# Five places instead of three for attention terms in the opening round, and one weight split moved from VectorE to GpSimd

## The chip, the cores and the metric

The kernel runs on one core of one Trainium2 chip. The metric is the time of one execution on the device in microseconds (us), as the median of several runs. The engines are named as in the profile: PE (TensorE), DVE (VectorE), ACT (ScalarE), POOL (GpSimd) and SP (SyncE, which here only issues transfers).

## What is computed

Sixteen sequences of 256 tokens with 512 features pass through two conditioned transformer layers. Cut to what matters:

```python
# layer 0: 16 heads of 32, keys and values through a latent of 128, window 64 in blocks of 128
proj = t_emb @ W_ada.T + b_ada                       # scale, shift of each sequence
h = layernorm(x) * (1 + scale) + shift
q = rope(h @ Wq.T);  c = h @ Wkd.T;  k = rope(c @ Wku.T);  v = c @ Wvu.T
x = x + softmax(q k^T / sqrt(32), masked) v @ Wo.T
# layer 1: 8 heads of 64, one key and value head, full attention, then the feed-forward part
h = rms(x) * ln1_w * (1 + cond @ ln1_tw.T)
x = x + softmax(rope(h Wq^T) rope(h Wk^T)^T / 8) (h Wv^T) @ Wo.T
h = rms(x) * ln2_w * (1 + cond @ ln2_tw.T)
out = x + (silu(h @ Wg.T) * (h @ Wu.T)) @ Wd.T       # 2048 wide
```

Matrices are multiplied as sums of fp16 products: each fp32 operand is split into a high half (its fp16 value) and a low half (what is left), and a product is three matmuls, high x high, high x low and low x high.

## The kernel before

The sequences go in pairs, eight rounds in all. A round runs layer 0 and layer 1 of its pair; the feed-forward part of the pair before is cut into parts that PE does between the attention steps of the round, by the table `PLAN`. Round 0, called the opening here, has no pair before it. In its place the opening prepares weights: each weight matrix is loaded into one of four staging slots in `inner_t` (or two more in `ring`), scaled by 64 and split into its two fp16 halves. `at_start(n)` is true for this round alone.

Each engine has its own instruction stream, in an order fixed by the Python code, and the streams meet in semaphores. Nothing is reordered on the chip.

Attention is done in units (table `UNIT`): 24 in layer 0, 16 in layer 1, for both sequences alternately. In layer 0 the units 0 to 7 are four heads of the first 128 queries against 128 keys each; the units 8 to 23 are two heads of the second 128 queries against 193 keys each. A unit j goes through these steps:

- PE: scores into one of four PSUM banks (in the opening preceded by a matmul that adds the mask, L1515); it needs the bank free, that is the low half of the unit that had it before
- DVE: the minimum of each row (`lows`, L1112 or L1121)
- ACT: exponentials with their sums (`exps`, L879), then the high half into `prob` (`prob_highs`, L888). Before the latter it waits in `turned_before` until the transpose that last read this place of `prob` has landed
- DVE: the low half into `prob` (`prob_lows`, L1128), and after it the minimum of unit j + 2
- SP: a DMA transpose of both halves out of `prob` (`turn_probs`, L583) into one of five places: four of `prob_t` and one in `x_mid` or `q_t`, once the product of unit j - 5 is done
- PE: the product with the values, four units later (`unit_values`, L1451 to L1453)

`prob` has `SLOTS = 3` places; unit g, counted through both layers, uses place g % 3. After the last unit of a sequence comes the normalisation (L1174, L1176), a transpose on PE, and the output projection with `wo0` or `wo1` (`finish`, `project`); DVE adds the result to x in `x_mid` (L1188), ACT sums squares (L1024) and POOL takes the root (`root`, L695 and L698), which DVE needs for the next layer.

The preparation of weights in the opening is dealt out as follows. `PIECE_OF` lists pieces of 512 columns: two for `kv`, four for `wq0`, four for `wo0`, one for `wkv1`. Pieces 0 to 5 have their high halves made by ACT, pieces from `DVE_PIECES = 6` on by DVE (L1396), and all low halves by DVE (L1400). `PIECES_AT` says before which step. The matrices of `BIG` are split by POOL alone (`big_some`): twelve instructions each, four for the high half (L780), four that scale the staged copy (L783) and four for the low half (L787); `SPLIT_AT` says at which step, and `big_split` counts those that are done, in the order of `BIG`. `split_wait` is how PE waits for a weight and SP for a stage that is to be loaded again: on `raw_split` for a matrix in pieces, on `big_split` for a big one.

`x_res` keeps the residual for the feed-forward part. It is written at the start of round 1, so in the opening it is unused but for four rows-of-16 scratch areas: `mod_copy[k]`, copies of the conditioning products k = 0 to 3 that PE then transposes. The matrices of these products are `ada0`, `ada1`, `tw1` and `tw2`.

## Time and profile before

| | us |
|---|---|
| median of 3 runs | 1775.21 |
| lowest, highest | 1773.86, 1775.33 |
| the profiled execution, its own time | 1777.36 |
| its span in the trace | 1775.60 |
| PE busy | 1705.9 (96%) |
| DVE busy | 1149.6 (65%) |
| ACT busy | 944.0 (53%) |
| POOL busy | 396.4 (22%) |

The span is the time from the first to the last instruction of the trace. Busy time is time in which an engine executes; register, branch and DMA-issuing instructions aren't counted. "Idle before <-X" behind an instruction says how long its engine had stood still and what ended it. The opening reaches from 0 to about 190 us of the span. In it, layer 0's attention units run from 50 to 99 us, layer 1's from 138 to 170.

### The profile page before, as it was taken

The page shows a single profiled execution, that of the slowest core. Times are in us where ns is not written, and L with a number is a line of the kernel's source. Part 1 is how long each engine was busy: PE and PEld are TensorE (multiplying, and loading weights), DVE is VectorE, ACT ScalarE, POOL GpSimd, SP SyncE. Part 2 cuts the span into 40 slices and gives each one's busy share as a digit, 9 for nine tenths or more (in the row PEclk, how much of TensorE's full clock was granted, in tenths as well). Part 3 has the DMA queues.
Part 4 walks back from the last instruction along what each step waited for, and adds up shares of the span by engine and source line. Part 5 has one row for each costly group of instructions (what it writes and reads, how often), then busy time and mean ns, then how long its engine had stood idle before and what let it go on. Part 6 is the DMA issues. An engine that isn't in the chain of part 4 may idle for free.

```text
span 1775.6 us, 37783 instructions
## 1 busy us (share of the span) xinstructions
PE 1705.9 (96%) x12440; PEld 930.8 (52%) x12440; DVE 1149.6 (65%) x2858; ACT 944.0 (53%) x2769; POOL 396.4 (22%) x556
## 2 busy tenths in 40 slices
PE   6676999999999999999999999999999999999999
PEld 2344545555555555555455555555555554555444
DVE  6758666676768667685676766686676856767320
ACT  3836466354755538464573547555384645735320
POOL 3438496021111011111110211110111111102120
PEclk9788999999999999999999999999999999999999
DMA  7876499353876449571793638763485817935310
GB/s 246 151 192 119 129 236 246 90 100 99 179 150 112 92 115 192 113 137 55 164 185 87 103 98 177 152 113 90 115 193 114 137 56 169 190 84 98 109 64 24
DMA packets 527227, 234.24 MB, mean 132 GB/s; under 512 B 476336, under 2 KB 493744, under 8 KB 527024
## 3 DMA queue, kind: packets, MB, share of 16 engines
q1 hardware_dynamic: 511472, 175.09, 49.6%
q10 hardware_dynamic: 15552, 56.63, 10.3%
q8 instruction: 104, 1.70, 0.4%
q14 instruction: 99, 0.81, 0.1%
HBM read 90.09 MB, written 16.78 MB: 60 GB/s over the span
## 4 chain that ended last, share of the span: by engine, by line
PE 75%; DMA 3%; DVE 3%; POOL 2%; issue 2%; ACT 1%; SPq 0%; DVEq 0%; ACTq 0%; POOLq 0%
PE up L1451 8%; PE up L1453 8%; PE up L1452 8%; PE gate L1451 8%; PE gate L1453 8%; PE gate L1452 8%; PE y L1453 4%; PE y L1451 4%; PE y L1452 4%; PE bank L1451 3%; PE bank L1453 3%; PE bank L1452 3%; DMA prob_t<-prob 2%; PE bank L1478 2%; PE bank L1486 1%
## 5 line engine op out<-in xcount | busy, mean ns | idle before, releaser
L879 ACT ACTIVATE bank<-bank,low 128x128 f32<-128x128 f32 (+2 forms) x768 | 302.5, 395 | 66.2 <-DVE low L1121 33.2
L704 POOL TENSOR_TENSOR inner_t<-inner,inner_t 128x512 f16<-128x512 f32 x128 | 150.9, 1179 | 640.0 <-ACT inner_t L1060 640.0
L1128 DVE TENSOR_TENSOR prob<-bank,prob 128x512 f16<-128x512 f32 (+1 forms) x320 | 202.8, 634 | 53.6 <-ACT prob L888 52.7
L888 ACT ACTIVATE prob<-bank 128x512 f16<-128x512 f32 (+1 forms) x320 | 178.3, 557 | 72.8 <-DMA prob_t<-prob 44.5
L1406 DVE SCALAR_TENSOR_TENSOR silu<-silu,gate 128x512 f32<-128x512 f32 x128 | 87.9, 686 | 170.9 <-ACT silu L1054 170.1
L1451 PE MATMUL gate<-mlp,ring 128*128 128x512 f16 x512 | 193.9, 379 | 1.6 <-DVE silu L1406 1.4
L1451 PE MATMUL up<-mlp,ring 128*128 128x512 f16 x512 | 193.8, 379 | 0.4 <-DVE inner L1416 0.4
L1453 PE MATMUL gate<-mlp,ring 128*128 128x512 f16 x512 | 194.0, 379 | 0.0
L1452 PE MATMUL gate<-mlp,ring 128*128 128x512 f16 x512 | 193.9, 379 | 0.0
L1453 PE MATMUL up<-mlp,ring 128*128 128x512 f16 x512 | 193.9, 379 | 0.0
L1452 PE MATMUL up<-mlp,ring 128*128 128x512 f16 x512 | 193.9, 379 | 0.0
L879 ACT ACTIVATION_READ_ACCUMULATOR bank<-bank,low 128x1 f32 x768 | 157.0, 204 | 0.0
L1054 ACT ACTIVATE silu<-gate 128x512 f32<-128x512 f32 x128 | 76.5, 598 | 125.0 <-PE gate L1453 124.6
L1117 DVE CUSTOM_DVE_ANT_0 bank<-bank,mask 128x128 f32<-128x128 f32 (+1 forms) x448 | 133.2, 350 | 1.1 <-PE bank L1522 1.0
L1024 ACT ACTIVATE work<-x_mid 128x512 f32<-128x512 f32 x64 | 40.3, 630 | 170.4 <-DVE x_mid L1188 170.4
L1060 ACT ACTIVATE inner_t<-inner 128x512 f16<-128x512 f32 x128 | 80.7, 631 | 92.7 <-DVE inner L1416 91.8
L1416 DVE SCALAR_TENSOR_TENSOR inner<-up,silu 128x512 f32<-128x512 f32 x128 | 88.2, 689 | 52.6 <-PE up L1453 42.8
L1451 PE MATMUL y<-v_hi,prob_t 128*128 128x32 f16 (+2 forms) x1024 | 109.3, 185 | 0.9 <-DMA prob_t<-prob 0.5
L1452 PE MATMUL y<-v_lo,prob_t 128*128 128x32 f16 (+2 forms) x1024 | 108.3, 184 | 0.0
L1453 PE MATMUL y<-v_hi,prob_t 128*128 128x32 f16 (+2 forms) x1024 | 108.2, 184 | 0.0
L1451 PE MATMUL bank<-wo_hi,act_hi 128*128 128x512 f16 x256 | 98.2, 383 | 1.3 <-DVE act_lo L1102 1.3
L1452 PE MATMUL bank<-wo_lo,act_hi 128*128 128x512 f16 x256 | 98.2, 384 | 0.0
(182 smaller groups left out, 4021.7 us busy)
## 6 DMA issues: line engine op xcount, KB each, us to landing
ring<-wgu_dram ACTq DMA_DIRECT2D x108, 512.0 KB, 3.9
x_in<-x_dram SPq DMA_DIRECT2D x18, 512.0 KB, 3.9
x_res<-x_mid SPq DMA_DIRECT2D x16, 512.0 KB, 3.1
wgu_dram<-ring SPq DMA_DIRECT2D x16, 512.0 KB, 3.6
out_dram<-x_res SPq DMA_DIRECT2D x32, 256.0 KB, 2.2
prob_t<-prob SPq DMA_TRANSPOSE x256, 3.5
inner_t<-wd_t_dram SPq DMA_DIRECT2D x4, 1024.0 KB, 9.3
ring<-wg_t_dram SPq DMA_DIRECT2D x16, 256.0 KB, 4.2
```

Source lines behind the costliest of these rows:

```text
L704: pool.tensor_tensor(inner_t[:, 1, f, :], inner[:], inner_t[:, 0, f, :], ALU.subtract).then_inc(inner_low, 1)
L879: ins = act.activation(bank_[:, at:at + wid], bank_[:, at:at + wid], ACT.Exp, bias=low[:, j % BANKS, k:k + 1], scale=-1.0, accum_out=total)
L888: act.activation(terms(prob[:, g % SLOTS, 0, :], layer, j), terms(work_bank[USE[f"unit{layer}", j] % BANKS][:], layer, j), ACT.Copy).then_ ...
L1054: act.activation(silu[:], gbank[:], ACT.Tanh, scale=0.5 / WS).then_inc(tanh_done, 1)
L1060: act.activation(inner_t[:, 0, f, :], inner[:], ACT.Copy).then_inc(inner_high, 1)
L1117: ins = dve.tensor_tensor_reduce(out=view, in0=view, in1=mask[:, 0:wid], scale=1.0, scalar=3.0e38, op0=ALU.add, op1=ALU.min, accum_out=low ...
L1128: dve.tensor_tensor(terms(prob[:, slot, 1, :], layer, j), terms(work_bank[USE[name] % BANKS][:], layer, j), terms(prob[:, slot, 0, :], lay ...
L1406: dve.scalar_tensor_tensor(silu[:], silu[:], 1.0, gbank[:], ALU.add, ALU.mult).then_inc(gated, 1)
L1416: dve.scalar_tensor_tensor(inner[:], ubank[:], 0.5 * HS / (WS * WS), silu[:], ALU.mult, ALU.mult).then_inc(inner_ready, 1)
L1451: pe.matmul(out_ap, left[0], right[0], start=start, stop=False)
L1452: pe.matmul(out_ap, left[0], right[1], start=False, stop=False)
L1453: return pe.matmul(out_ap, left[1], right[0], start=False, stop=stop)
```

## The change

Six edits. (1) In the opening alone there are five places for the terms, `OPEN_SLOTS = 5`: the three of `prob` and two more in the first half of `x_res`, seen as fp16 (`more_prob`). `prob_place` gives the place of a unit, `turned_before` waits by five or three. In round 1, the first units wait for the transposes of the opening that last read places 0 to 2. (2) POOL zeroes the two new places as well (`prob_clear` counts to 2). (3) `mod_copy` uses the second half of `x_res` alone, so that k = 0 and 2 share a place, as do 1 and 3. (4) `wo0` is no longer in `PIECE_OF`; piece 6 is `wkv1`, still before `unit0_18`. (5) `wo0` is in `BIG`, between `wq1` and `wo1`, and POOL splits all three at the step `fill0.0`. (6) `big_views` knows the new key.

```diff
-PIECES_AT = {"first": range(0, 2), "lat.0": range(2, 6), "unit0_9": range(6, 7), "unit0_11": range(7, 8),
-             "unit0_14": range(8, 9), "unit0_16": range(9, 10), "unit0_18": range(10, 11)}
-BIG = ["wq1", "wo1", "wd2", "wd0", "wd1", "wd3"]
-SPLIT_AT = {"fill0.0": BIG[:2], "out0a.0": BIG[2:3], "unit1_0": BIG[3:4], "unit1_4": BIG[4:5],
-            "unit1_6": BIG[5:]}
+PIECES_AT = {"first": range(0, 2), "lat.0": range(2, 6), "unit0_18": range(6, 7)}
+BIG = ["wq1", "wo0", "wo1", "wd2", "wd0", "wd1", "wd3"]
+SPLIT_AT = {"fill0.0": BIG[:3], "out0a.0": BIG[3:4], "unit1_0": BIG[4:5], "unit1_4": BIG[5:6],
+            "unit1_6": BIG[6:]}
...
-        SLOTS, TURNED = 3, LAG + 1
+        SLOTS, OPEN_SLOTS, TURNED = 3, 5, LAG + 1
...
-        mod_copy = [x_res[0:SEQS, k // TILES, k % TILES, :] for k in range(4)]
+        mod_copy = [x_res[0:SEQS, 1, k % TILES, :] for k in range(4)]
...
-                ("wq0", wq0, 4), ("wo0", wo0, 4), ("wkv1", None, 1)) for p in range(pieces)]
+                ("wq0", wq0, 4), ("wkv1", None, 1)) for p in range(pieces)]
...
+        more_prob = x_res[:, 0].rearrange("p t d -> p (t d)").bitcast(F16).rearrange(
+            "p (m a k) -> p m a k", m=OPEN_SLOTS - SLOTS, a=2)
+
+        def slots(n):
+            return OPEN_SLOTS if at_start(n) else SLOTS
+
+        def prob_place(n, g):
+            slot = g % slots(n)
+            return prob[:, slot] if slot < SLOTS else more_prob[:, slot - SLOTS]
+
         def turned_before(eng, n, g):
-
-            if g < SLOTS:
-                n, last = (n[0], n[1] - 1), max(k for k in range(sum(UNITS))
-                                                if k % SLOTS == g % SLOTS)
+            if at_start(n) and g < OPEN_SLOTS:
+                return
+            if g < slots(n):
+                n = (n[0], n[1] - 1)
+                last = max(k for k in range(sum(UNITS)) if k % slots(n) == g)
             else:
-                last = g - SLOTS
+                last = g - slots(n)
             need(eng, prob_in[last % TURNED], turned_count(n, last))
...
                 sp.dma_start(turned_place(g).rearrange("p a b q -> p (a b) q"),
-                             prob[:, g % SLOTS].rearrange("p a k -> p (a k)"),
+                             prob_place(n, g).rearrange("p a k -> p (a k)"),
...
             pool.memset(prob[:], 0.0).then_inc(prob_clear, 1)
+            pool.memset(more_prob, 0.0).then_inc(prob_clear, 1)
...
-                act.activation(terms(prob[:, g % SLOTS, 0, :], layer, j),
+                act.activation(terms(prob_place(n, g)[:, 0, :], layer, j),
...
-            act.wait_ge(prob_clear, 1)
+            act.wait_ge(prob_clear, 2)
...
-                name, slot = (f"unit{layer}", j), unit_index(layer, j) % SLOTS
+                name, place = (f"unit{layer}", j), prob_place(n, unit_index(layer, j))
```

Where the instructions stand. On DVE, in layer 0 of the opening, this stood from unit 11's piece to unit 13's terms; `wo_hi` and `wo_lo` are the two halves of `wo0`:

```order
L1176 TENSOR_TENSOR work<-y,inv 128x512
L1396 TENSOR_SCALAR wo_hi<-inner_t 128x512
L1400 SCALAR_TENSOR_TENSOR wo_lo<-inner_t,wo_hi 128x512
L1128 TENSOR_TENSOR prob<-bank,prob 128x2x193
L1112 TENSOR_REDUCE low<-bank 128x2
L1174 RECIPROCAL inv<-sums 128x16
L1176 TENSOR_TENSOR work<-y,inv 128x512
L1128 TENSOR_TENSOR prob<-bank,prob 128x2x193
L1112 TENSOR_REDUCE low<-bank 128x2
L1380 TENSOR_SCALAR gain<-gate,ln_w 128x16 x8
L1128 TENSOR_TENSOR prob<-bank,prob 128x2x193
L1112 TENSOR_REDUCE low<-bank 128x2
```

and this stands there now (line numbers of the changed kernel):

```order
L1185 RECIPROCAL inv<-sums 128x16
L1187 TENSOR_TENSOR work<-y,inv 128x512
L1139 TENSOR_TENSOR prob<-bank,prob 128x2x193
L1123 TENSOR_REDUCE low<-bank 128x2
L1185 RECIPROCAL inv<-sums 128x16
L1187 TENSOR_TENSOR work<-y,inv 128x512
L1139 TENSOR_TENSOR prob<-bank,prob 128x2x193
L1123 TENSOR_REDUCE low<-bank 128x2
L1391 TENSOR_SCALAR gain<-gate,ln_w 128x16 x8
```

The two instructions of a piece are gone between the normalisation and the low half of unit 11; the same happens before units 9, 14 and 16.

On POOL, at the step `fill0.0` of the opening, this stood between the last table of layer 1 and the angles (CAST) of the next round; the name `wo` stands here for `wo1`:

```order
L780 TENSOR_SCALAR wq_hi<-inner_t 128x512 x4
L783 TENSOR_SCALAR inner_t<-inner_t 128x512 x4
L787 TENSOR_TENSOR wq_lo<-inner_t,wq_hi 128x512 x4
L780 TENSOR_SCALAR wo_hi<-inner_t 128x512 x4
L783 TENSOR_SCALAR inner_t<-inner_t 128x512 x4
L787 TENSOR_TENSOR wo_lo<-inner_t,wo_hi 128x512 x4
L798 CAST posf<-pos 128x4
```

and now the same form twice, first `wo0`, then `wo1`:

```order
L790 TENSOR_SCALAR wq_hi<-inner_t 128x512 x4
L793 TENSOR_SCALAR inner_t<-inner_t 128x512 x4
L797 TENSOR_TENSOR wq_lo<-inner_t,wq_hi 128x512 x4
L790 TENSOR_SCALAR wo_hi<-inner_t 128x512 x4
L793 TENSOR_SCALAR inner_t<-inner_t 128x512 x4
L797 TENSOR_TENSOR wo_lo<-inner_t,wo_hi 128x512 x4
L790 TENSOR_SCALAR wo_hi<-inner_t 128x512 x4
L793 TENSOR_SCALAR inner_t<-inner_t 128x512 x4
L797 TENSOR_TENSOR wo_lo<-inner_t,wo_hi 128x512 x4
L808 CAST posf<-pos 128x4
```

Twelve instructions have come in ahead of the split of `wo1`.

On SP, the transposes of the terms of layer 0 from unit 1 on took their source from `prob` alone:

```order
L583 DMA_TRANSPOSE prob_t<-prob 128x8x128 x3
L583 DMA_TRANSPOSE x_mid<-prob 128x8x128
L583 DMA_TRANSPOSE prob_t<-prob 128x8x128 x4
L583 DMA_TRANSPOSE x_mid<-prob 128x8x128
L583 DMA_TRANSPOSE prob_t<-prob 128x8x128 x4
L583 DMA_TRANSPOSE x_mid<-prob 128x8x128
```

and now take two in five from `x_res`:

```order
L593 DMA_TRANSPOSE prob_t<-prob 128x8x128 x2
L593 DMA_TRANSPOSE prob_t<-x_res 128x8x128
L593 DMA_TRANSPOSE x_mid<-x_res 128x8x128
L593 DMA_TRANSPOSE prob_t<-prob 128x8x128 x3
L593 DMA_TRANSPOSE prob_t<-x_res 128x8x128
L593 DMA_TRANSPOSE x_mid<-x_res 128x8x128
L593 DMA_TRANSPOSE prob_t<-prob 128x8x128 x3
L593 DMA_TRANSPOSE prob_t<-x_res 128x8x128
```

Neither their number nor their targets have changed.

## Rows read from the trace of the kernel before

**Rows 1.** The page, part 2: PE in 40 slices, busy tenths.
```profile
PE   6676999999999999999999999999999999999999
```

**Rows 2.** Stretches; columns: us, PE, PEld, DVE, ACT, POOL busy, PEclk, DMA share, GB/s.
```profile
66.00:99.00 33.00, 23.40 (x284) 15.49 (x282) 26.85 (x61) 25.08 (x93) 4.51 (x11) 0.60 0.86 141
99.00:116.00 17.00, 12.40 (x89) 6.13 (x87) 5.96 (x11) 4.08 (x10) 11.04 (x18) 0.98 0.98 315
...
138.00:170.00 32.00, 20.23 (x228) 15.27 (x227) 29.40 (x51) 25.49 (x82) 30.89 (x42) 0.74 0.77 137
```

**Rows 3.** Groups of 66 to 99 us: busy, mean ns, idle before and its releaser.
```profile
L879 ACT ACTIVATE bank<-bank,low 128x193 f32<-128x193 f32 x32 | 12.6, 393 | 3.3 <-DVE low L1112 3.1
L1112 DVE TENSOR_REDUCE low<-bank 128x2 f32<-128x386 f32 x16 | 8.8, 549 | 0.0
L888 ACT ACTIVATE prob<-bank 128x386 f16<-128x386 f32 x16 | 8.0, 499 | 3.9 <-DMA x_mid<-prob 2.2 <-DMA prob_t<-prob 1.3
```

**Rows 4.** Timeline of ACT: start us, us, instruction, idle before.
```profile
70.11 0.50 ACT L888 ACTIVATE prob<-bank 128x386 f16<-128x386 f32 x1 [0.63 <-DMA prob_t<-prob]
...
71.44 0.50 ACT L888 ACTIVATE prob<-bank 128x386 f16<-128x386 f32 x1
...
91.60 0.50 ACT L888 ACTIVATE prob<-bank 128x386 f16<-128x386 f32 x1
```

**Rows 5.** Timeline of DVE, units 10 to 13 of layer 0.
```profile
73.58 0.67 DVE L1368 COPY x_res<-up 16x512 f32<-16x512 f32 x1
...
75.99 0.42 DVE L1396 TENSOR_SCALAR wo_hi<-inner_t 128x512 f16<-128x512 f32 x1
...
77.05 0.56 DVE L1128 TENSOR_TENSOR prob<-bank,prob 128x386 f16<-128x386 f32 x1
...
77.98 0.24 DVE L1174 RECIPROCAL inv<-sums 128x16 f32<-128x16 f32 x1
...
78.87 0.56 DVE L1128 TENSOR_TENSOR prob<-bank,prob 128x386 f16<-128x386 f32 x1
...
79.80 1.22 DVE L1380 TENSOR_SCALAR gain<-gate,ln_w 128x16 f32<-128x16 f32 x8
```

**Rows 6.** Transposes by SP: landing after issue, and a queries' one in the timeline.
```profile
DMA to landing us min/median/max: 3.0/3.2/4.7
...
51.81 3.34 SPq L614 DMA_TRANSPOSE q_t<-x_mid  x1
```

**Rows 7.** Timeline of POOL up to layer 0's last scores.
```profile
1.43 2.66 POOL L830 MEMSET prob<- 128x3072 f16 x1
5.99 0.19 POOL L798 CAST posf<-pos 128x4 f32<-128x4 int32 x1 [1.90 <-DMA freq<-freq_c_dram]
...
56.67 2.37 POOL L780 TENSOR_SCALAR wo_hi<-inner_t 128x512 f16<-128x512 f32 x4
...
61.34 4.49 POOL L787 TENSOR_TENSOR wo_lo<-inner_t,wo_hi 128x512 f16<-128x512 f32 x4
93.65 0.19 POOL L798 CAST posf<-pos 128x4 f32<-128x4 int32 x1 [27.82 <-PE bank L1522]
```

**Rows 8.** The end of layer 0: timelines of SP, PE, POOL.
```profile
92.89 7.47 SPq L583 DMA_TRANSPOSE prob_t<-prob  x4
...
97.11 0.21 PE L1451 MATMUL y<-v_hi,prob_t 128*128 128x32 f16 x1 [0.52 <-DMA prob_t<-prob]
...
106.37 2.37 POOL L780 TENSOR_SCALAR wd_hi<-inner_t 128x512 f16<-128x512 f32 x4 [5.54 <-DMA inner_t<-wd_t_dram]
```

**Rows 9.** Timeline of DVE with GpSimd at work and idle.
```profile
60.60 0.69 DVE L1128 TENSOR_TENSOR prob<-bank,prob 128x512 f16<-128x512 f32 x1 [0.74 <-ACT prob L888]
...
66.68 0.69 DVE L1128 TENSOR_TENSOR prob<-bank,prob 128x512 f16<-128x512 f32 x1 [0.74 <-ACT prob L888]
```

**Rows 10.** Layer 1: waits of ACT (us, times, longest), timeline of POOL.
```profile
ACT prob L888 <- DMA prob_t<-prob: 2.0, 3, 1.2
...
184.31 0.19 POOL L695 TENSOR_SCALAR shifted<-squares 128x2 f32<-128x2 f32 x1 [5.93 <-ACT work L1024]
```

More of the change, by code:

```diff
@@ L453, in big_views @@
             slot = staged(key)
-            w, at = ((wq1, 0) if key == "wq1" else (wo1, 0) if key == "wo1" else
-                     (wd, int(key[-1]) * CH))
+            whole = {"wq1": wq1, "wo0": wo0, "wo1": wo1}
+            w, at = (whole[key], 0) if key in whole else (wd, int(key[-1]) * CH)
             return [(slot[:, c * D:(c + 1) * D], flat(w[half])[:, (at + c) * D:(at + c + 1) * D])
@@ L1125, in prob_lows @@
             def prob_lows(n, layer, j):
-                name, slot = (f"unit{layer}", j), unit_index(layer, j) % SLOTS
+                name, place = (f"unit{layer}", j), prob_place(n, unit_index(layer, j))
                 need(dve, hi_done, count(n, HI_USES, HI_USE[name] + 1))
-                dve.tensor_tensor(terms(prob[:, slot, 1, :], layer, j),
+                dve.tensor_tensor(terms(place[:, 1, :], layer, j),
                                   terms(work_bank[USE[name] % BANKS][:], layer, j),
-                                  terms(prob[:, slot, 0, :], layer, j),
+                                  terms(place[:, 0, :], layer, j),
                                   ALU.subtract).then_inc(prob_split, 1)
```

## The prediction

> **What bounds the kernel now.** First the row of PE on the page [rows 1]: from the fifth of 40 slices on PE is busy 90% and more, in the first four 60 to 70%. All later rounds put feed-forward work between the attention steps; the opening round has none, so only there a chain of waits can set the time. Everything that the change touches lies in it. Then the stretches [rows 2]: in 66 to 99 us, the second half of layer 0's attention, DVE is busy 26.85 of 33 us, ACT 25.08, PE 23.40 (at 0.60 of its clock). No engine is full: they pass units to each other. Then what ACT waits for there [rows 3]: 3.1 us for DVE's minima before its exponentials, and 2.2 + 1.3 = 3.5 us for a transfer before it may write the high half, that is for a free place of `prob`.
>
> **The pace of a unit.** Units 8 to 23 have two heads each. The highs of units 8 and 9 start at 70.11 and 71.44 [rows 4]: 1.33 us, of which the pair of exponentials (with what follows) takes 0.94 and the high half 0.39 until the next may start. That is ACT's floor. On DVE the low half and the next minimum take 77.98 - 77.05 = 0.93 [rows 5], 0.47 each; the minimum's 0.55 us [rows 3] and a step of 0.03 pass before ACT may start, and the low half starts 0.53 after its high. From unit 8 (70.11) to unit 20 (91.60) before took 21.49 us where the floor is 12 x 1.33 = 15.96: 5.5 us of waits.
>
> **The change part by part.**
> 1. DVE loses four pieces of `wo0`. One is 77.05 - 75.99 = 1.06 us [rows 5], so four are 4.24. They stand before units 9, 11, 14 and 16. What stays on DVE: the copy of conditioning rows (0.67, 0.60 until the next may start) before 10, a normalisation (78.87 - 77.98 = 0.89) behind 10 and behind 11, the gains before 13 (1.22, some 1.26 until the next) [rows 5], and the piece of `wkv1` before 18 (an estimate of 1.2: the elements of one `wo0` piece in four instructions instead of two).
> 2. Five places. A place is held from the high half to the landing: 0.53 + 0.59 + 3.1 to 3.2 (landing after issue: 3.0 at least, 3.2 median, 4.7 at most) [rows 6] = 4.3 us, so three places allow a unit each 1.43 us, above the floor of 1.33, and one slow landing (4.7) makes it 1.9. Five allow 0.86 and, even with a slow landing, 1.2. These waits go: 0.63 us at unit 8 and 2.9 us behind it. They aren't simply added to part 1, since with the pieces gone everything runs closer to the places and with the places freed closer to DVE.
>
> I replay units 8 to 20 with the durations above. Rule: a pair of exponentials starts 0.39 after the last high or 0.58 after its minimum started, the later; high = pair + 0.94; low half = high + 0.53 or when DVE is free; then the minimum of the unit two ahead, then what DVE has extra. Fed with what happened before (pieces, places as they landed) it puts the high of unit 20 at 91.58, the trace has 91.60 [rows 4], so the rules hold. Without pieces and place waits the highs of 8 to 15 start at 69.5, 70.8, 72.2, 73.5, 74.9, 76.7, 78.5, 80.7: ACT keeps its floor up to 11; then the two normalisations and the gains make it lose 0.07, 0.47, 0.47 and 0.87. Units 16 to 19 follow at the floor (86.0), the `wkv1` piece costs unit 20 0.67: 88.0. Gain at that high: 3.6 us, from both parts (with three places and no pieces the same replay gives 89.1, gain 2.5; with five places and the pieces 90.4, gain 1.1).
>
> What matters is the landing of unit 20's transpose: PE waits for it until 97.11 [rows 8], and behind it come the output projection with its additions. After: low half at 88.55, issue at 89.28, landing after 3.1 at 92.4, against 97.06: 4.7 earlier. Unit 20's transpose was one of the slow ones (it went out at 92.89 and took 4.2); if it is slow again the gain is 3.6. I take 4.2 for the end of layer 0's attention. The second chain out of it goes along: SP issues the load of `wd2` behind the last transpose, GpSimd waits 5.54 us for it until 106.37 [rows 8] and gives the roots that layer 1 starts with only behind that split, 9.2 us later [rows 7], at about 115.6. By the replay the last transpose goes out 4.7 us earlier. The angles on GpSimd, released by the last scores at 93.65 [rows 7], end before those 5.54 us of waiting, and still do when all moves together.
>
> 3. GpSimd takes `wo0` over. One such split lasts from 56.67 to 61.34 + 4.49 = 65.83: 9.2 us [rows 7]. GpSimd is idle for 27.82 us before 93.65 [rows 7], so the split of `wo1` moves from 65.8 to 75.0 and all is done 13 us before the angles (now about 89) and 17 before PE wants `wo0` (92.8). Cost 0; without that cover it would be the full 9.2. The loads into the freed stages wait for big splits that are then 20 us old. Zeroing the two new places is 2048 of the 3072 elements that took 2.66 us [rows 7]: 1.77 us, from 4.09 to 5.9, inside the 1.90 us that GpSimd waits for the frequencies until 5.99. Cost 0; at the most the 1.77, if none of it were hidden.
> 4. The conditioning rows go to the other half of `x_res`, the same instructions: 0.
>
> At one place the notes speak against part 3. DVE's low halves of `prob` take 0.69 us at 60.60, with GpSimd at work, and 0.69 at 66.68, with GpSimd idle [rows 9]: no loss. The Trainium skill (SBUF — State Buffer, "Who interferes with whom") says that a DVE instruction with two SBUF inputs blocks against a GpSimd one that reads SBUF; the low half has one input in PSUM, so that by the rule too it is free, and the trace agrees. The pieces that leave DVE had both inputs in SBUF, and would be hit.
>
> 5. Layer 1 (138 to 170 us) has five places too. ACT waited 2.0 us for places there [rows 10], but DVE is busy 29.40 of 32 us [rows 2], with the next round's statistics and normalising in it, so a high that comes sooner waits for DVE. Bounds 0 and 1.0; I take 0.2, by DVE's row. Behind it GpSimd's own chain (splits of `wd` and the first chunks) has 5.93 us of slack before the root of 184.31 [rows 10], and it starts earlier with the rest.
> 6. Rounds 1 to 7 have the same instructions; they start earlier by the whole gain.
>
> **The sum.** 4.2 + 0.2 = 4.4 us. The profiled execution took 1777.36 us (span 1775.60 and 1.76 around it), 2.15 above the median of the runs; it gives 1772.96. From the median 1775.21 I forecast 1770.8, -0.25%. Measurement can tell about 0.2% (3.6 us) from no change.
>
> **Rivals.**
> A. The transposes become the bound. Before, a unit took 1.79 us on average, after it 1.54. The query transposes, twice the size, were issued back to back in up to 3.34 us each [rows 6], so 1.67 for one of a unit is the upper bound, 1.28 (1.23 of issue and a step) the lower; I lean to the lower, since the highs of 8 and 9 were followed by landings without growing delay. At 1.67, unit 20's landing is 12 x 1.67 = 20.0 behind unit 8's (73.7): 93.7, the gain 3.4, and with some of it lost again behind it 3.0: 1772.2.
> B. The gain is taken back behind the attention. Layer 1's start hangs on the load of `wd2` (5.54 us of GpSimd idle [rows 8]) and the first feed-forward chunks on GpSimd's splits. If one of these chains is not shifted but only catches up, half of the 4.4 is left: 1773.0.
> C. Slower: PE's clock. It was granted at 0.60 in 66 to 99 and at 0.98 in 99 to 116 [rows 2], where the four projections stand. Should the denser, shifted units leave it at 1.2 GHz there, the 12.40 us of PE busy would double, +12.2 at the most; the 4.6 idle us of the stretch take some of it, I put +9: 1779.8. It decides from 4.4 us lost, that is when over a third of that work runs at the low level. Against it: the work there is the same, as dense as before, and before it got the high level right after a stretch at 0.60.
> D. More than forecast: the clock comes up sooner. The first projection starts right behind 97.11 [rows 8], two us ahead of the stretch with 0.98; with 0.3 us of low level in that stretch (2% of 17 us, twice) some 2.3 to 2.7 us run at half speed and cost 1.2 to 1.3. With as much again in layer 1's and shorter waits in the units: 2.5 more, 1768.3.
> That the places aren't used is no rival of its own: the order of transposes shows sources in `x_res` from unit 3 on.
>
> **Chances.** Forecast (3.4 to 5.6 us, so 1769.6 to 1771.8) 0.50; A 0.17; B 0.16; C 0.05; D 0.12. Faster by over 0.2% takes the forecast's mass nearly whole, D, and nothing of A and B: 0.60. Within 0.2%: A, B and a small part of the forecast, 0.35. Slower: 0.05, C. Range: 1767.5 to 1774.5.
>
> **What would show it.** ACT's waits for a transfer before the high halves gone in 66 to 92 us; waits for minima still 2 to 2.5 us; no `wo_hi` on DVE and unit 20's high at about 88; PE's wait for unit 20's transpose over at 92.4 to 93.5; `wo1` split by 75; layer 1's first unit about 4.4 us before 140.8, the first root of its end 4.6 before 184.31, the span 1771.2. Wrong: if transposes land more than 3.6 us after issue through the stretch (A), if GpSimd's root of about 115.6 moves by less than 3 (B), if the granted clock in the projections is below 0.9 (C).

## The result, and the profile after

| kernel | median us | runs | against before, 95% | profiled execution (span) |
|---|---|---|---|---|
| before | 1775.27 | 6 | | 1777.36 (1775.60) |
| changed | 1765.82 | 6 | 0.9947 [0.9937, 0.9957] | 1765.57 (1763.8) |

Faster by 9.4 us, 0.53%. The forecast was 4.4, with 1767.5 as the lower end. The runs below show that the priced steps were about right, and that two things came on top that the prediction had not priced: the rounds themselves got shorter, and the end of layer 1 in the opening did, where TensorE's granted clock was low in some records.

The page of the changed kernel, TensorE in 40 slices, against [rows 1]; the second to fourth slice, most of the opening, went up by one tenth each:

```profile
PE   6787999999999999999999999999999999999999
```

Stretches of the changed kernel, columns as in [rows 2], moved forward with the work. In 66 to 95 the granted clock is 0.60 as before, the work is done in 29 us instead of 33; the projections behind it have 0.98 as before; DMA is at 1.02 of its engines where it was at 0.86.

```profile
66.00:95.00 29.00, 22.85 (x271) 14.42 (x270) 22.87 (x53) 23.96 (x91) 12.88 (x23) 0.60 1.02 165
95.00:112.00 17.00, 12.36 (x91) 6.17 (x89) 6.67 (x12) 4.08 (x10) 12.05 (x19) 0.98 1.03 332
134.00:165.00 31.00, 22.69 (x224) 16.63 (x225) 27.70 (x49) 25.27 (x81) 30.43 (x42) 0.61 0.79 141
```

Groups of 66 to 95, against [rows 3]. The exponentials wait 2.1 us for minima (3.1 before). The highs go to two buffers now, and neither group waits for a transfer any more (3.5 us before). In each row: busy, mean ns, idle before and its releaser:

```profile
L890 ACT ACTIVATE bank<-bank,low 128x193 f32<-128x193 f32 x32 | 12.6, 395 | 2.1 <-DVE low L1123 2.1
L1123 DVE TENSOR_REDUCE low<-bank 128x2 f32<-128x386 f32 x16 | 8.8, 549 | 0.0
L899 ACT ACTIVATE prob<-bank 128x386 f16<-128x386 f32 x9 | 4.5, 500 | 0.3
L899 ACT ACTIVATE x_res<-bank 128x386 f16<-128x386 f32 x7 | 3.5, 499 | 0.2
```

ACT's timeline, against [rows 4], the highs of units 8 to 11, 14 and 20. The replay had 69.5, 70.8, 72.2, 73.5 for the first four, 78.5 for unit 14 and 88.0 for unit 20; the whole stands 0.8 earlier, since unit 0 did (51.78 against 52.67, which varies from run to run), and the distances are the forecast's:

```profile
68.66 0.50 ACT L899 ACTIVATE x_res<-bank 128x386 f16<-128x386 f32 x1
70.00 0.50 ACT L899 ACTIVATE x_res<-bank 128x386 f16<-128x386 f32 x1
71.33 0.50 ACT L899 ACTIVATE prob<-bank 128x386 f16<-128x386 f32 x1
72.66 0.50 ACT L899 ACTIVATE prob<-bank 128x386 f16<-128x386 f32 x1
...
77.69 0.50 ACT L899 ACTIVATE x_res<-bank 128x386 f16<-128x386 f32 x1
...
87.23 0.50 ACT L899 ACTIVATE prob<-bank 128x386 f16<-128x386 f32 x1
```

The end of layer 0, against [rows 7, 8]: PE has unit 20's transpose at 92.86 (97.11 before). GpSimd zeroes the two places in 1.80 us under the wait for the frequencies, which is gone; wo1 is split by 74.1; the split of wd2 starts at 100.91 (106.37), 5.5 earlier, and the roots stand right behind it, at 110.44 for the first `rstd` (115.89):

```profile
92.86 0.21 PE L1462 MATMUL y<-v_hi,prob_t 128*128 128x32 f16 x1 [0.49 <-DMA prob_t<-prob]
```

```profile
4.03 1.80 POOL L841 MEMSET x_res<- 128x2048 f16 x1
5.78 0.19 POOL L808 CAST posf<-pos 128x4 f32<-128x4 int32 x1
...
69.58 4.50 POOL L797 TENSOR_TENSOR wo_lo<-inner_t,wo_hi 128x512 f16<-128x512 f32 x4
...
100.91 2.37 POOL L790 TENSOR_SCALAR wd_hi<-inner_t 128x512 f16<-128x512 f32 x4 [4.44 <-DMA inner_t<-wd_t_dram]
...
110.44 0.70 POOL L708 TENSOR_TENSOR rstd<-shifted,minus_half 128x2 f32<-128x2 f32 x1
...
176.45 0.19 POOL L705 TENSOR_SCALAR shifted<-squares 128x2 f32<-128x2 f32 x1 [3.69 <-ACT work L1035]
```

The last row is the first surprise. It is the root of layer 1's end, 184.31 in [rows 10], 4.6 earlier by the forecast, 7.86 by the trace. The second is behind the opening.

Marks of four of the profiled executions, in us. "Units" is from the high of unit 0 to that of unit 20, "chain" from there to the first `rstd`, "layer 1" from the high of unit 24 to that of unit 39, "end" from there to the first feed-forward tanh of the opening, "five rounds" from the first tanh of the third round to that of the eighth:

| kernel | units | chain | layer 1 | end | first tanh | five rounds |
|---|---|---|---|---|---|---|
| before | 38.94 | 24.29 | 28.48 | 27.57 | 196.21 | 1034.2 |
| before, again | 39.09 | 24.54 | 28.48 | 27.52 | 195.77 | 1032.8 |
| changed | 35.45 | 23.21 | 28.36 | 25.36 | 188.27 | 1029.6 |
| changed, again | 35.49 | 23.22 | 28.37 | 25.35 | 188.62 | 1030.4 |

The units gain 3.5, the chain 1.1 to 1.3, layer 1's units 0.1, its end 2.2, the start -0.2 to 0.9, five rounds 2.4 to 4.6. "Before" and "changed" below mean these two kernels; a ratio is the time against the kernel before in runs beside it, with its 95% interval.

### The profile page after: what moved, and what is told of

Read it like the earlier page. It is cut to its first block, busy times and chain, and to the rows that moved or that the text cites. A ratio compares the mean times of both kernels' runs of the same rounds, so it can differ in the third digit from the quotient of the medians.

```text
span 1763.8 us, 37787 instructions
## 1 busy us (share of the span) xinstructions
PE 1704.7 (97%) x12440; PEld 930.8 (53%) x12440; DVE 1146.8 (65%) x2850; ACT 944.7 (54%) x2769; POOL 407.7 (23%) x569
## 3 DMA queue, kind: packets, MB, share of 16 engines
q10 hardware_dynamic: 15552, 56.63, 10.4%
## 4 chain that ended last, share of the span: by engine, by line
PE 82%; DMA 2%; DVE 1%; ACT 1%; issue 1%; SPq 0%; DVEq 0%; ACTq 0%
PE up L1462 9%; PE up L1463 9%; PE up L1464 9%; PE gate L1462 9%; PE gate L1464 9%; PE gate L1463 9%; PE y L1464 4%; PE y L1463 4%; PE y L1462 4%; PE bank L1462 3%; PE bank L1463 3%; PE bank L1464 3%; DMA prob_t<-prob 2%; PE bank L1489 2%; PE bank L1533 2%; PE bank L1497 1%
## 5 line engine op out<-in xcount | busy, mean ns | idle before, releaser
L1139 DVE TENSOR_TENSOR prob<-bank,prob 128x512 f16<-128x512 f32 (+1 forms) x304 | 192.7, 634 | 42.0 <-ACT prob L899 41.0
L899 ACT ACTIVATE prob<-bank 128x512 f16<-128x512 f32 (+1 forms) x304 | 169.5, 557 | 58.3 <-DMA prob_t<-prob 38.9
L1462 PE MATMUL gate<-wd_hi,inner_t 128*128 128x512 f16 x256 | 97.0, 379 | 0.6 <-DVE silu L1417 0.6
```

The lines of the kernel that those rows point to most:

```text
L899: act.activation(terms(prob_place(n, g)[:, 0, :], layer, j), terms(work_bank[USE[f"unit{layer}", j] % BANKS][:], layer, j), ACT.Copy).then ...
L1139: dve.tensor_tensor(terms(place[:, 1, :], layer, j), terms(work_bank[USE[name] % BANKS][:], layer, j), terms(place[:, 0, :], layer, j), AL ...
L1462: pe.matmul(out_ap, left[0], right[0], start=start, stop=False)
```

## Experiments

### One part alone, and both kernels again

```
s1_split_only:  SLOTS, OPEN_SLOTS = 3, 3             (wo0 on GpSimd, no new places)
s1_places_only: PIECES_AT, BIG, SPLIT_AT as before   (five places, wo0's pieces on VectorE)
```

> The kernel before, unchanged, profiled a second time. Ratio to before 1.000. It says how far two profiles of one kernel differ inside the opening. Theory A (the surplus of the 9.4 us over the 4.4 that I forecast lies in where PE's clock falls in the projections and in layer 1's end, and that pattern belongs to the kernel): unit 20's high again at 91.6 us within 1, the end of the opening (first tanh of the feed-forward part) at 196.2 within 1, with stretches at the low clock within 178 to 192 us again. Theory B (the surplus is chance of single executions): the first tanh moves by 2 us or more between two profiles of this same kernel.

Measured: 1775.55, ratio 0.9996 [0.9988, 1.0005]; first tanh at 195.77, 0.4 from the first record, as theory A had it.

> The changed kernel, unchanged, profiled a second time. Ratio 0.9947 (9.4 us less). Theory A: first tanh again at 188.3 us within 1, clock high from 160 to 180 us again. Theory B: it comes 2 us or more later, nearer to 190 to 191.

Measured: 1766.18, 0.994 [0.9927, 0.9953]; the difference repeats.

> The changed kernel with three places in the opening too: only the split of wo0 is on GpSimd. My replay of layer 0's attention gives unit 20's high 2.5 us before 91.6 (89.1) where the full change gives 3.6; ACT's waits for a place stay, 2 us and more in the units. If the parts just add as replayed, 3 to 4 us of total gain at the end of the opening (theory A: plus what the clock gives or takes, 0 to 3). Rival: if the GpSimd split carries the whole gain, 9 us (ratio 0.995).

Measured: 1770.17, 0.9967 [0.9955, 0.9979]. Units 36.78, 2.2 less than before (replay 2.5); chain 24.37; end 25.07; five rounds 1029.4. The whole gained 5.6 us by the medians.

> The changed kernel with wo0 split by DVE in four pieces again: only the five places are left. The replay gives unit 20's high 1.1 us earlier (90.4), ACT's waits for a place 0, its waits for DVE's minima 4 us or more. Total 1 to 2 us (ratio 0.999) by the replay, theory A: plus what the clock gives. Rival: if places carry the whole gain, 0.995.

Measured: 1772.01, 0.9981 [0.9972, 0.999]. Units 38.42, 0.6 less (replay 1.1); end 24.98; five rounds 1033.0. In the units each part is near what the replay said, and together they give a little more than their sum (0.6 + 2.2 against 3.5). But the 0.6 is not clear of chance: four records of the kernel before run from 38.4 to 39.4. The whole gained 3.7 us by the medians, where 1 to 2 were expected; most of it, 2.6, is in the end of layer 1, which is looked at below. Only where wo0 had left VectorE the rounds were short.

### The number of places

```
-        SLOTS, OPEN_SLOTS, TURNED = 3, 5, LAG + 1
+        SLOTS, OPEN_SLOTS, TURNED = 3, 4, LAG + 1
```

> The changed kernel with four places in the opening instead of five. The replay of the prediction (a place is held 4.3 us, so four allow a unit each 1.08 us, below the floor of 1.33; only a landing of 4.7 us or more makes it 1.4 to 1.5): the high of unit 0 to the high of unit 20 takes 35.5 to 36.0 us, where five places took 35.45 and three took 36.78; the time is within 0.5 of five places, about 1766.3. Rival (each further place gives its share): half way, 36.1 or more, and the time 1768. If what is saved in the rounds behind the opening hangs on VectorE's program being eight instructions shorter, it is the same here as with five places: five rounds in 1029.4 to 1030.4 us.

Measured: 1766.55, 0.9952 [0.9939, 0.9965]; units 35.90; five rounds 1029.2. The replay holds: the fourth place gives all that can be seen, since seven records of openings with five places (the changed kernel and those below with nothing but instructions added behind its opening) run from 35.4 to 36.0.

### TensorE's clock

Unread matmuls of 128x512 in the opening, where TensorE waited:

```
s2_before_warm, layer 1 only:
+                warm(n, 4 * layer)    (before its heads; 2 behind them, 5 behind the projections, 3 in the fill)
s2_after_warm:
+                    if layer or j >= 12:
+                        warm(n, 2)    (in each unit; 4, 2, 9 or 5 around the projections, 3 in the fill)
```

> The kernel before, with matmuls added on TensorE whose product nothing reads (128x512, one pass each): four before layer 1's first projections of the opening, two behind them, five behind the second projections and three between the two halves of the fill, so that TensorE is busy where it waited. Theory (part of the gain is TensorE's clock in the last part of layer 1 of the opening): before, the records have stretches at a granted 0.5 from 178.3 and from 188.5 us, and from the high of unit 39 to the first feed-forward tanh it took 27.5 us, against 25.0 to 25.4 in all three kernels with a changed opening. With TensorE kept busy those stretches go, that distance falls to 25.0 to 26.0 and the whole is 1.5 to 2.5 us shorter, ratio 0.9986 to 0.9992. Rival (the distance shrank because waits for data moved, the clock is only an accompaniment): the distance stays at 27.5 or grows by the time of the added work (up to 3), the ratio 1.000 to 1.002.

Measured: 1775.64, 0.9999 [0.9991, 1.0008]. The end took 25.57 instead of 27.57, as the theory had it; the whole did not get shorter. That the matmuls did it is not shown: the fourth record of the kernel before, below, has 25.35 without them.

Stretches at the end of layer 1, of the kernel before and with the matmuls, columns as in [rows 2]: granted 0.86 and 1.00. In the first one the engine had waited 1.01 and 0.67 us for work before the projections.

```profile
171.00:183.00 12.00, 10.11 (x73) 5.04 (x72) 4.60 (x9) 2.64 (x6) 7.29 (x9) 0.86 0.25 23
```

```profile
171.00:183.00 12.00, 11.56 (x87) 5.92 (x86) 5.06 (x9) 3.36 (x8) 7.29 (x10) 1.00 0.32 23
```

> The changed kernel with the same kind of unread matmuls in both layers of the opening: two in each unit from unit 12 on, four, two and nine (five in layer 1) around the projections, three in the fill. If TensorE's clock in the opening is worth time beyond what the changed kernel already gets: the stretches at 0.5 from 112.6 and in 136.5 to 160.4 us get shorter, and the time falls by 1 to 3 us against the changed kernel, to 1763 to 1765 (ratio to before 0.9925 to 0.9938). Rival (attention there is bound by VectorE and ScalarE, TensorE at either level keeps up, and the added matmuls delay the scores): no gain or a loss of 1 to 3, 1766 to 1769.

Measured: 1774.29, 0.9999 [0.9987, 1.0011], 8 us slower than the changed kernel; the rival was right in sign (its 1766 to 1769 was too low), but not in its reason. The clock came up (66 to 95: 0.94 instead of 0.60), the units took 36.1 instead of 35.45, VectorE's first addition of a projection to x came 8.8 behind unit 20's high instead of 9.9, the chain 23.56, so none of that reached layer 1, whose start hangs on GpSimd. The end took 26.66, the added matmuls in the way. The first tanh was only 1.2 later; the loss is in the rounds, where no instruction was added: five took 1037.9. So the place of the code in the rounds comes under suspicion.

Does the slow end belong to the kernel before? Two more records of it:

> The kernel before, unchanged. If the 2.2 us at the end of layer 1 belong to the kernel before: unit 39's high to the first tanh takes 27.4 to 27.7 us again, with granted clock stretches at 0.5 near 178 and 188. If they belong to the execution: it takes 25.0 to 25.6 in at least one of the two new records, with the low stretches elsewhere. Five rounds take 1032.5 to 1034.5 us in either case.

> The kernel before once more, with the same two expectations: 27.4 to 27.7 us from unit 39's high to the first tanh if the slow end of layer 1 belongs to this kernel, 25.0 to 25.6 in this record or the third if it belongs to the execution.

Measured: end 27.90 in the third, 25.35 in the fourth (five rounds 1031.9 and 1032.1; each a single run, 1775.91 and 1774.16). The same stretch of the fourth record, with the projections at the high level, though TensorE had waited 0.79 and 0.67 us for work before them:

```profile
170.00:182.00 12.00, 10.29 (x81) 5.48 (x80) 5.70 (x11) 2.70 (x7) 8.58 (x11) 1.00 0.36 42
```

Of five records of this layer 1 (the fifth is the kernel before with memsets, below, 25.35) three had the slow end, of the eleven changed kernels without added matmuls none (24.97 to 25.36). So it depends on the execution, and with these counts the change seems to make it rarer, for a reason that no run shows: on average 26.7 against some 25.1, 1.6 us.

### The place of VectorE's loop

VectorE's program ahead of its loop over the rounds is eight instructions shorter in the changed kernel: the four pieces of wo0, two each. So all code of the loop lies eight instructions earlier. The runs push it back, first with waits that are always satisfied, then with one-column memsets that nothing reads, in both kernels:

```
             layer0((None, 0), None)
             layer1((None, 0), None)
+            for k in range(8):                         (s3; s4: 4 and 16; s2: dve.wait_ge(const_in, 32))
+                dve.memset(pad[:, k:k + 1], 0.0)
             with dve.Fori(0, NP - 1) as i:
```

> The changed kernel with eight waits that are always satisfied added to VectorE's program between the opening and the loop over the rounds, so that the loop's instructions stand where they stood in the kernel before (which has eight more instructions on VectorE ahead of them). Theory (the rounds themselves became shorter by some 0.6 us each because VectorE's loop is placed elsewhere in memory, and its instructions arrive otherwise): five rounds take 1032.7 to 1034 us again, as before and with places alone, instead of 1029.4 to 1030.4, and the time is 1.5 to 3.5 us above the changed kernel, 1767.5 to 1769.5. Rival (the rounds differ by how the opening hands over to them, or by chance): five rounds stay at 1029.4 to 1030.4, the time within 0.5 of 1766.

Measured: 1768.1, 0.9956 [0.9944, 0.9969], five rounds 1029.2. The rounds stayed short; the code had moved less than meant, too (the block of the table below came at 164.5 to 165.1), so this run doesn't decide on the theory, though its rounds came out as the rival had them.

> The changed kernel with eight one-column memsets (nothing reads them) on VectorE between the opening and the first round of the loop, so that VectorE's program ahead of the rounds is as long as in the kernel before. Satisfied waits had left the places of VectorE's constant gaps in the rounds as they were; real instructions should move them. Theory (about 0.6 us a round of the gain come from where VectorE's loop stands, since its instructions arrive with gaps of 0.35 us at fixed places): the gaps of a round stand where they stood before (at its 34th, 158th and 414th instruction, not the 160th and 421st), five rounds take 1032.7 to 1034 us, the time is 1767.5 to 1769.5, 1.5 to 3.5 above the changed kernel. Rival (the gaps move but are hidden, the rounds differ by phase or chance): five rounds in 1029.4 to 1030.4, the time 1765.8 to 1767.

Measured: 1770.16, 0.9968 [0.9956, 0.998], five rounds 1033.6; on VectorE the pauses of 0.35 us that come in every round are ahead of the 158th and 414th instruction again, as before. The theory holds.

> The kernel before with the same eight memsets at the same place, so that its loop stands eight instructions further on. Theory (the place of VectorE's loop sets part of a round): the gaps of 0.35 us move to yet other instructions and five rounds take another time than 1032.7 to 1034.2, by 1 us at least, in either direction. Rival: five rounds stay in 1032.7 to 1034.2, the time within 1 of the kernel before (0.5 us of memsets).

Measured: 1771.88, 0.9979 [0.997, 0.9988], five rounds 1029.5. The kernel before gets 3 us faster from eight instructions more; that is more than half of the 5.0 us that the change gave over the forecast, without the change.

> The changed kernel with four one-column memsets on VectorE ahead of the rounds (eight made it 4.1 us slower, and the kernel before 3.1 us faster with them). If VectorE's loop has only the two placements seen so far, this is one of them: five rounds take 1029.2 to 1030.4 us and the time is 1766 to 1767, or 1034 us and 1769.5 to 1770.5. If each added instruction costs by itself, it is in the middle: 1768.

Measured: 1769.86, 0.9955 [0.994, 0.997]; five rounds 1031.5, four of them 206.0 to 206.2 and one 207.6. Its opening ended late (first tanh 191.70), with a granted 0.75 in 95 to 112. By itself it decides nothing. (Beside this kernel and the three others that were run with it, those with 16 memsets, with four small matmuls and with wo0 split first, the kernel before took 1778.09, and 1774.8 to 1775.7, also medians, beside the rest; so the ratios compare them.)

> The changed kernel with sixteen such memsets. Place: the kernel before plus eight stands where the changed kernel stands plus sixteen, and had short rounds. So five rounds take 1029 to 1030.4 us, the constant gaps of a round are at its 160th instruction again, and the time is 1766 to 1767.5, faster than with eight. Added work or length as such: at least as slow as with eight, 1770 or more.

Measured: 1766.7, 0.9946 [0.9931, 0.996], five rounds 1029.5. Sixteen cost nothing (the changed kernel has 0.9947 and 0.994) where eight cost 4 us: it is the place, not the work.

What the place does can be seen in the transfers. Part 3 of the page (before) has two queues that bring the instructions themselves:

```profile
q8 instruction: 104, 1.70, 0.4%
q14 instruction: 99, 0.81, 0.1%
```

That is 16 KB a packet on q8 and 8 KB on q14. The Trainium skill (Runtime: NRT & Kernel Launch, "Instruction fetch mechanics") says that an engine's program is fetched in blocks by a DMA queue of its own while it runs, at a cost that is mostly hidden; the packets are there, the cost here was not hidden. In the rounds each block comes at nearly the same point every time. Of the 12 or 13 that q14 brings in a round, four move with VectorE's padding (in one round of the changed kernel and of the one with eight memsets: from 15.4 to 10.7, 87.6 to 85.4, 129.6 to 128.1 and 166.9 to 163.1 us behind the round's first tanh), the others by at most 1.4 us, so it seems that q14 brings more than VectorE's. The last of the four lies near the end of layer 1 at (us behind the round's first tanh):

| kernel | q14's block | longest distance of two highs there | five rounds |
|---|---|---|---|
| before, four records | 163.2 to 164.8 (once 162.2) | 3.4 to 4.2 | 1031.9 to 1034.2 |
| places alone | 162.2 to 164.0 | 3.5 to 4.25 | 1033.0 |
| changed + 8 | 162.9 to 164.9 | 3.4 to 3.8 | 1033.6 |
| changed + 8 satisfied waits | 164.5 to 165.1 | 2.4 to 3.2 | 1029.2 |
| changed + 4 | 164.7 to 165.8 | 2.5 to 3.0 | 1031.5 |
| changed, two records | 166.7 to 167.8 | 2.4 to 3.3 | 1029.6, 1030.4 |
| changed + 16 | 161.1 to 161.4 | 2.8 to 3.1 | 1029.5 |
| before + 8 | 161.3 to 161.7 | 2.4 to 3.1 | 1029.5 |

ScalarE waits there for a unit's transpose into `q_t`, issued 159.9 to 161.7 us behind the round's first tanh. In the first three rows of the table the block comes 2.0 to 4.1 us after this issue, so with the transpose under way, and the transpose lands 4.9 to 5.8 us after its issue; in the other five the block comes at most 1.6 or at least 4.4 us after it, and the landing takes 4.0 to 4.8. Over the five rounds ScalarE waits 11.4 to 12.3 us for these transposes in the kernel before, 11.5 with places alone and 10.4 in changed + 8, and 5.8 to 7.1 in the others. In one round (before, changed + 8, changed, before + 8; the changed kernel's is one of its longest):

```profile
989.61 0.60 ACT L888 ACTIVATE prob<-bank 128x512 f16<-128x512 f32 x1 [1.99 <-DMA q_t<-prob]
```

```profile
983.12 0.60 ACT L900 ACTIVATE prob<-bank 128x512 f16<-128x512 f32 x1 [1.91 <-DMA q_t<-prob]
```

```profile
980.05 0.60 ACT L899 ACTIVATE prob<-bank 128x512 f16<-128x512 f32 x1 [1.66 <-DMA q_t<-prob]
```

```profile
986.12 0.60 ACT L889 ACTIVATE prob<-bank 128x512 f16<-128x512 f32 x1 [0.93 <-DMA q_t<-prob]
```

TensorE, full in the rounds, has no slack for it: it waits for the low half behind that high. Over the five rounds, columns us, times, longest, before and changed + 8; the changed kernel, the one with 16 and before + 8 have no such row (the second record of the changed kernel has one of 0.2 us):

```profile
PE bank L1486 <- DVE prob L1128: 2.0, 6, 0.6
```

```profile
PE bank L1500 <- DVE prob L1140: 1.2, 6, 0.3
```

The place as a cause is shown, by eight instructions in both directions and by sixteen. That this block delays the transpose is an inference: the two go together in the 12 records of the table, but the three other blocks that move were not told apart from it. The 1.2 to 2.1 us of TensorE's waits are less than the 2 to 5 us by which the rounds differ; the rest stands in its busy time (1030.2 to 1031.9 us of the five rounds in the first three rows, 1029.4 to 1030.0 in changed, changed + 16 and before + 8), and no row says why. Three kernels with warming matmuls don't fit. The kernel before with them has the block at 162.7 to 164.0, but distances of 2.6 to 3.3 and landings of 4.2 to 4.3 us, and rounds of 1032.7. The changed kernel with them and the one further below keep the changed kernel's block (166.8 and later), and have rounds of 1037.9 and 1034.5. There TensorE's program had grown too; in the one with 1037.9, q8's block of this stretch had moved from 161.2 to 162.1 up to 167.1 to 168.4.

```
s4_tensor_longer, behind TensorE's layer 1 of the opening:
+            for k in range(4):
+                pe.matmul(ubank[:, 0:8], wkd[0][:, 0, :], flat(wkd[0])[:, 0:8], start=True, stop=True)
```

> The changed kernel with four small matmuls (8 columns, unread; with their weight loads eight instructions) on TensorE behind its opening. If only the place of VectorE's loop matters: 1766 to 1766.8, rounds as in the changed kernel. If TensorE's loop has such a property too (the kernels with added matmuls had longer rounds): 1 us or more slower, 1767.5 to 1771.

Measured: 1769.83, 0.9962 [0.9948, 0.9976], but in the profiled execution 1030.2 for five rounds and a span of 1765.2. The ratio speaks for a loss of some 3 us against the changed kernel's 0.9947 and 0.994 (the intervals just overlap), the record, which is the fastest of its seven runs, doesn't show where; it stays open whether TensorE's place matters the same way.

### The chain on GpSimd, and a faster version

```
-LOADS_AT = {..., "out0a.0": ["wd2"], ...}
+LOADS_AT = {..., "unit0_10": ["wd2"], ...}    (s4_wd2_first: "unit0_2", and BIG = ["wo0", "wq1", "wo1", ...])
-SPLIT_AT = {"fill0.0": BIG[:3], "out0a.0": BIG[3:4], ...}
+SPLIT_AT = {"fill0.0": BIG[:4], ...}
```

> The changed kernel with the load of wd2 behind unit 10's transpose (its stage is free from the split of wo0 on) instead of behind the attention, and its split on GpSimd right behind wo1's. Theory (what opens layer 1 is GpSimd's chain: load of wd2, its split of 9.2 us, then the roots; the output projections end earlier): the first root comes 0.5 to 1.2 us sooner behind the high of unit 20, at 22.0 to 22.7 instead of 23.2, and GpSimd's later splits get 9 us of room; time 1764.8 to 1765.8. Rival (1 MB beside the transposes makes them land late, and the units wait for their values or places): the highs of units 12 to 20 take 1 to 4 us more, the time 1766.5 to 1770.

Measured: 1769.89, 0.9971 [0.9959, 0.9983]. The chain took 21.11, 2.1 less, so layer 1's start did hang on wd2. But the units took 41.23 instead of 35.45: the rival, and dearer than it said. The expectation was wrong on the stage, which is wo1's and not wo0's, but wo1 was split by then. SP's timeline: the load goes out at 75.13, the transposes behind it are drawn out, and ScalarE waits for one:

```profile
75.13 0.37 SPq L515 DMA_DIRECT2D inner_t<-wd_t_dram  x1
75.59 6.00 SPq L593 DMA_TRANSPOSE prob_t<-prob  x2
81.69 2.01 SPq L593 DMA_TRANSPOSE prob_t<-x_res  x1
```

```profile
84.26 0.50 ACT L899 ACTIVATE prob<-bank 128x386 f16<-128x386 f32 x1 [2.17 <-DMA prob_t<-prob]
```

> The same, with two unread matmuls on TensorE in each unit from 16 on and four before the second heads of layer 0, to have its clock up when the projections of layer 0 begin. Where units 12 to 23 and the projections were kept busy before, the first addition came 8.8 us behind the high of unit 20 instead of 9.9, but GpSimd's chain hid that. Theory (with that chain gone the clock's 1.1 us reach the end): first root 21.0 to 21.8 us behind the high of unit 20, time 1763.7 to 1764.8, the fastest yet. Rival (added matmuls delay scores, or the rounds get longer as they did with the kernel that had many of them): no gain over the kernel without them, 1766 or more.

Measured: 1773.31, 0.9989 [0.998, 0.9998]. The chain took 20.00, 1.1 less again, with a granted 1.00 instead of 0.89 in 98 to 115 us and the first addition 8.7 behind unit 20's high instead of 9.8: the clock's gain does reach layer 1 once GpSimd's split is out of the way, and the first root waits for ScalarE's squares. Units 40.46, and the rounds long, 1034.5, one of them 209.9.

> The changed kernel with GpSimd splitting wo0 before wq1 and wo1, so that wd2's load can go out behind unit 2's transpose, ahead of the dense units (behind unit 10's it made units 0 to 20 take 41.2 us instead of 35.5). Theory: the load meets the units with one head, where places are free, and costs at most 1.5 us there; the first root comes 21.1 us behind the high of unit 20, as it did then, instead of 23.2, and the time is 1765.3 to 1766.5. Rival (the transposes behind it land late whatever the unit): units 0 to 20 take 38 us or more, the time 1767 to 1770.

Measured: 1785.97, 1.0049 [1.0032, 1.0065]. Both expectations missed the cause: the high of unit 0 came at 59.78 instead of 51.78. wo0's split has nothing to wait for but its load, so GpSimd began it at 22.41, beside VectorE's first normalisations and splits, and both engines' instructions got longer. Groups of VectorE in 20 to 38 us, the changed kernel and this one:

```profile
L1411 DVE SCALAR_TENSOR_TENSOR wq_lo<-inner_t,wq_hi 128x512 f16<-128x512 f32 x4 | 2.5, 684 | 0.0
...
L1096 DVE CAST act_hi<-work 128x512 f16<-128x512 f32 x4 | 1.7, 422 | 0.2 <-ACT work L866 0.2
```

```profile
L1411 DVE SCALAR_TENSOR_TENSOR wq_lo<-inner_t,wq_hi 128x512 f16<-128x512 f32 x4 | 6.3, 1636 | 0.0
...
L1096 DVE CAST act_hi<-work 128x512 f16<-128x512 f32 x4 | 3.1, 776 | 0.2 <-ACT work L866 0.2
```

The load was not issued early either: SP stood in front of it until wo1 was split (74.21), and all transposes from unit 3 on behind it, so that the units took 43.3. No version beats the changed kernel.

## Why the prediction was wrong

By its own steps, with what each was worth:

- Units (parts 1 and 2), 3.6 at the high of unit 20: 3.5 in both pairs of records (3.2 between the averages of all records of the two openings). Three places without pieces 2.5: 2.2; five with pieces 1.1: 0.6; four as good as five: yes. Right.
- End of layer 0's attention, 4.2 taken out of 3.6 to 4.7: PE's wait for the landing ended 97.11 - 92.86 = 4.25 earlier, but 0.9 of that had been there at unit 0, which leaves 3.4 (3.7 in the second pair). The transpose was slow again (4.3 us), for which the prediction had 3.6. So the 4.2 as a landing was too much, and the 4.25 agrees by luck. What opens layer 1 is the second chain, and the first `rstd` moved by 5.45, less the same 0.9: 4.6 (4.9 in the second pair). The prediction had put that chain 4.7 earlier and still summed by PE's 4.2; mis-sized by 0.4 to 0.7.
- GpSimd takes wo0 over, cost 0: right, the cover was 15.20 us still at the angles. Zeroing, 0: right. (Of the pieces that left VectorE only the low halves, L1400, have both inputs in SBUF, not the high halves as well.)
- Layer 1, 0.2 of 0 to 1.0: 0.1. Right.
- The end of layer 1 had no term. Rival D named "as much again in layer 1's" and shorter waits, 2.5 in all with a chance of 0.12; in the pair of records it is 2.2, on average of all records 1.6. A second term that was missing.
- Part 6, "rounds 1 to 7 have the same instructions; they start earlier by the whole gain". This is the step that failed. The instructions are the same, their place is not: with VectorE's loop put back to where it stood, the changed kernel takes 1770.16, 4.8 us under before by the medians and 5.7 by the ratio (0.9968, that is 3.6 to 7.8), an interval that holds the forecast of 4.4; and the kernel before moved by eight gains 3.1 by the medians and 3.7 by the ratio (0.9979, 2.1 to 5.3). With both loops where the rounds are short (before + 8 against changed + 16) the ratios differ by 0.0033, 5.9 us. The rounds' share in the records is 2.8 us over five rounds, between four records of the kernel before (1031.9 to 1034.2) and two of the changed one.
- The sum of what was measured (units, chain, layer 1's units, its end, rounds): 3.5 + 1.2 + 0.1 + 1.6 + 2.8 = 9.2, against 9.4. The terms come from different sets of records, and each is good to half a us at best; that they meet so well is partly luck.
- Rivals A (landings up to 4.7 us, but median 3.3 in 66 to 92, under its sign of 3.6, and no growing delay) and B (`rstd` moved by more than 3) were wrong. C did not come in this pair. But the clock in the projections is a matter of the execution too, in both kernels. In 99 to 116 us the four records of the kernel before and the one with memsets were granted 0.98, 0.99, 0.85, 0.81 and 0.82, and the high of unit 24 came 48.6 to 49.1 us behind that of unit 20 in all five. In 95 to 112 the two records of the changed kernel were granted 0.98 and 0.97, and that distance was 47.3; in the five that have the same opening and something added behind it 0.75 to 0.85, and it was 48.4 to 50.2. So the 1.1 to 1.3 us of the chain were seen only where the clock was high, and with the chain shortened the low clock costs up to 3 us there, where the kernel before hid it.

## What to carry over

An edit ahead of a loop moves the loop's code; where the loop is full, try the same kernel with some harmless instructions more or fewer before an edit is given the gain, or blamed for the loss. When a replay of the waits fits the kernel before, it can be trusted for its own stretch (here to 0.1 to 0.5 us in the units), and the error is in what lies outside it. Of two chains that both start from the place of the change, the sum goes by the one that the next stage waits for.

## Not expected of the hardware

- The instruction blocks on the queues: 8 and 16 KB packets at fixed points of a round, and 3 to 4 us a run by where VectorE's loop lies.
- GpSimd beside VectorE: a split with both inputs in SBUF took 1636 ns instead of 684, a cast 776 instead of 422, and GpSimd's own group 4.10 instead of 2.37 us. The Trainium skill (SBUF — State Buffer, "Who interferes with whom") has it that the two exclude each other on a shared pair of ports, when an instruction of VectorE has two inputs in SBUF or runs in one of its two-port modes; these rows agree, and give a price, which the kernel before didn't show. No run tells the ports from another cause.
- A 1 MB load behind a transpose made the next two take up to 6.00 us together on SP and cost 5.8 us over ten units.
